# Zeroing a stage's semaphores in one block on five engines instead of one SyncE block per group

## The reference

```python
xn = _layernorm(x)
s = _L0_attn_ref(xn, ...)      # 16 heads of 16: W = (1e-4 + distance(Q, K)) ** -2, normalised, times V, gated
g = _silu(_L0_ffn_ref(xn, ...))  # ternary weights plus a low-rank part, squared ReLU, hidden 1024
x = x + s * g
xn = _layernorm(x)
s = _L1_attn_ref(xn, ...)      # W = (1 - arccos(cosine(Q, K)) / pi) ** 16, normalised, times V
g = _silu(_L1_ffn_ref(xn, ...))  # ternary weights, ReLU
x = x + s * g
```

## Time and profile before

| | us |
|---|---|
| median of 3 runs | 6679.3 |
| lowest and highest of them | 6676.99, 6679.74 |
| the profiled execution | 6678.16 |
| its span, first to last instruction | 6676.4 |
| ACT busy | 6177.6 (93%) |
| DVE busy | 5850.0 (88%) |
| POOL busy | 4185.5 (63%) |
| PE busy | 3870.0 (58%) |

### The profile page before, as it was taken

One profiled execution on the slowest core, in us unless ns is written; L12 is line 12 of the kernel. 1 busy time (PEld: TensorE's weight loads), 2 busy tenths in 40 slices (PEclk: granted clock), 3 DMA queues, 4 the chain that ended last, 5 costly groups with the idle time before them and its releaser, 6 DMA issues. The chain is left out here.

```text
span 6676.4 us, 49638 instructions
## 1 busy us (share of the span) xinstructions
PE 3870.0 (58%) x17072; PEld 1359.1 (20%) x17072; DVE 5850.0 (88%) x5940; ACT 6177.6 (93%) x1923; POOL 4185.5 (63%) x1127
## 2 busy tenths in 40 slices
PE   5777777777776764544454454444545444454545
PEld 2222222222222420111111121111112111111213
DVE  7867677767767679999999999999999999999996
ACT  3699999999999349999999999999999999999996
POOL 0399999999996006565565656556565656556563
PEclk8899999999998875566656665555656566665657
DMA  4311111111111420000000000000000000000003
GB/s 150 97 27 22 25 27 26 27 27 20 27 25 49 165 86 6 15 8 9 8 14 10 8 15 8 9 8 15 9 8 15 8 9 8 15 9 8 15 6 103
DMA packets 448852, 191.93 MB, mean 29 GB/s; under 512 B 348038, under 2 KB 429849, under 8 KB 446698
## 3 DMA queue, kind: packets, MB, share of 16 engines
q1 hardware_dynamic: 448618, 188.89, 11.1%
HBM read 112.52 MB, written 76.28 MB: 28 GB/s over the span
## 5 line engine op out<-in xcount | busy, mean ns | idle before, releaser
L1322 POOL TENSOR_TENSOR work<-work 128x1776 f32<-128x1776 f32 (+3 forms) x696 | 2149.0, 3088 | 55.3
L1114 PE MATMUL psS<-q_stack,k_stack 96*128 96x512 bf16 x2048 | 1034.0, 607 | 1761.0 <-DVE work L1230 1695.4
L981 POOL TENSOR_TENSOR work<-work 128x4096 f32<-128x4096 f32 x249 | 1737.7, 7013 | 152.6 <-ACT work L886 152.6
L896 DVE TENSOR_SCALAR work<-psS 128x1024 f32<-128x1024 f32 x1024 | 1198.1, 1218 | 555.0 <-PE psS L798 553.6
L1319 POOL TENSOR_SCALAR work<-work 128x1776 f32<-128x1776 f32 (+2 forms) x174 | 290.8, 1671 | 1990.6 <-ACT work L1204 1983.3
L1225 DVE TENSOR_SCALAR work<-psS 128x1024 f32<-128x1024 f32 x1024 | 1205.0, 1218 | 42.2 <-PE psS L1114 18.1
L1230 DVE TENSOR_TENSOR work<-psS,work 128x1024 f32<-128x1024 f32 x1024 | 1200.8, 1214 | 0.0
L1236 DVE SCALAR_TENSOR_TENSOR work<-work 128x2048 f32<-128x2048 f32 x512 | 1139.1, 2283 | 30.2 <-ACT work L1200 30.2
L1196 ACT ACTIVATE work<-work 128x2048 f32<-128x2048 f32 (+2 forms) x259 | 910.7, 3565 | 53.9 <-DVE work L1230 53.8
L1204 ACT ACTIVATE work<-work 128x6144 f32<-128x6144 f32 (+2 forms) x174 | 907.8, 5217 | 32.1 <-DVE work L1236 32.1
L1200 ACT ACTIVATE work<-work 128x2048 f32<-128x2048 f32 (+1 forms) x343 | 916.0, 2741 | 1.0
(11 more groups left out here) (139 smaller groups left out, 3398.0 us busy)
## 6 DMA issues: line engine op xcount, KB each, us to landing
qk_parts<-work SPq DMA_DIRECT2D x64, 384.0 KB, 3.3
q_stack<-qk_parts SPq DMA_DIRECT2D x384, 64.0 KB, 2.3
k_stack<-qk_parts SPq DMA_DIRECT2D x384, 64.0 KB, 2.3
xT_store<-work SPq DMA_DIRECT2D x2, 4096.0 KB, 15.8
v_store<-work SPq DMA_DIRECT2D x16, 512.0 KB, 3.3
v_tile<-v_store SPq DMA_DIRECT2D x64, 128.0 KB, 2.8
ffn_in<-xT_store SPq DMA_DIRECT2D x64, 128.0 KB, 2.7
y_store<-ffn_out SPq DMA_DIRECT2D x64, 128.0 KB, 2.4
```

What stands on the lines that cost most here:

```text
L896: nc.vector.tensor_scalar(lane(g)[:, 0, half * 1024:(half + 1) * 1024], m.psS[half][:, :], ZERO_SHIFT, None, ALU.max).then_inc(s_gd, 1)
L981: nc.gpsimd.tensor_tensor(lane(g, 2), lane(g, 2), lane(g, 2), ALU.mult).then_inc(s_wp, 1)
L1114: last = nc.tensor.matmul(m.psS[half][:, q * 512:(q + 1) * 512], m.k_stack[b][0:ROWS, kt * P:(kt + 1) * P], m.q_stack[b][0:ROWS, c:c + 512 ...
L1322: nc.gpsimd.tensor_tensor(part, part, part, ALU.mult).then_inc(s_pp, 1)
```

## The change

`sems` no longer registers a clear. It adds its semaphores to a list of the stage (`Phase.made`), and `Phase.block()` registers a single `clear` for the whole list just before it opens the stage's block. `clear` deals the list out: every fifth semaphore to SP, and likewise to DVE, ACT, PE and POOL, in one block. All seven stage functions use `Phase` in place of `ExitStack`.

```diff
+class Phase(ExitStack):
+    def __init__(self, nc):
+        super().__init__()
+        self.nc, self.made = nc, []
+    def block(self):
+        self.callback(clear, self.nc, self.made)
+        return self.enter_context(self.nc.Block())
 def sems(nc, ctx, prefix, *names):
     made = [ctx.enter_context(nc.semaphore(f"{prefix}_{n}")) for n in names]
-    ctx.callback(clear, nc, made)
+    ctx.made.extend(made)
     return made
...
     with nc.Block() as block:
         @block.sync
         def _(sp):
-            for s in made:
+            for s in made[0::5]:
                 sp.sem_clear(s)
+        @block.vector
+        def _(dve):
+            for s in made[1::5]:
+                dve.sem_clear(s)
+        @block.scalar
+        def _(act):
+            for s in made[2::5]:
+                act.sem_clear(s)
+        @block.tensor
+        def _(pe):
+            for s in made[3::5]:
+                pe.sem_clear(s)
+        @block.gpsimd
+        def _(pool):
+            for s in made[4::5]:
+                pool.sem_clear(s)
...
-    with ExitStack() as ctx:
+    with Phase(nc) as ctx:
...
-        block = ctx.enter_context(nc.Block())
+        block = ctx.block()
```

## The result

The changed kernel takes 6664.19 us (median of 17 runs) against 6678.56 us for the kernel before (17 runs): 14.4 us less. The ratio is 0.9978, with a 95% interval from 0.9971 to 0.9985. The profiled execution's span went from 6676.4 to 6661.9 us, 14.5 us less. One of the 17 runs of the changed kernel took 8298.85 us (granted clock 1.0), and one of the later runs of the kernel before took 8308.47 us; the ratios are taken without these two.

The account below looks back on a forecast made before the run. Eleven stretches between stages, 22.48 us with no engine at work, were taken to lie on the path. Handshakes of 3.85 us plus PE's clears of 3.7 us replace them, 14.9 us less: 6664.4 us, range 6660.0 to 6669.5 us.

Parts of the forecast that it names:

- What bounds: Eleven stretches between stages, 22.48 us with no engine at work; each microsecond cut there is one off the end.
- Rival 4: Stretches of norm and output stages hidden behind older work; about 6 us of the gain go, 6670.4 us; chance 0.03.
- The prices on SP: In the clear blocks between stages, 0.25 us per block besides its clears and 0.056 us per clear on SP.
- The floor: Least time of a clear block's handshake, however little SP does: 0.35 us each, 3.85 us for eleven blocks.
- The price of a clear on PE: PE, taken to finish each clear block last: 0.090 us per clear, 41 clears, 3.7 us.
- rival 1: Clears dear on PE or another engine: 0.18 us each gives 6668.1 us; verdict line crossed at 0.13 us; chance 0.14.
- The sum: Eleven stretches: 3.85 + 3.7 = 7.55 us in place of 22.48 us, 14.9 us less, median 6664.4 us.
- Rival 2: Shorter PE gaps keep TensorE's clock up at two stage boundaries; another 3.8 us won, 6660.6 us; chance 0.06.
- Rival 3: Jumps into and out of new clear bodies wait for code, 22 x 2.3 = 50.6 us; 6715.0 us; chance 0.03.
- The argument from the earlier trace: Against rival 3: DVE's first-norm-stage loops jump back repeatedly while the instruction queue moves a single packet in 50 us.
- The rule in the Trainium skill: About 51 ns per always-taken branch; 22 branches in a row on one engine would add 1.1 us; not added.

Follow-up runs that it names:

- merging alone: Against the kernel before: one clear block behind each stage, SP zeroing all 219 semaphores alone; 6671.21 us, ratio 0.9990.
- without PE: Against the changed kernel: each stage's semaphores dealt over four engines, SP, DVE, ACT and POOL; 6666.25 us in a single run.
- dealing out alone: Against the kernel before: its 40 clear blocks kept, each dealt over five engines; 6675.0 us, ratio 0.9995.

## Why the prediction was right, point by point

**What bounds.** The stretches were taken to be wholly on the path. Six kernels with stretches from 0.9 to 30 us bear it out. Against the 22.5 us of before, the stretches changed by -21.6, -13.5, -6.9, -3.1 and +7.7 us, and the medians by -23.1, -14.4, -7.2, -3.4 and +7.9 us. The medians move a little more each time, by 0.2 to 1.5 us. That lies within the intervals, and I leave it open. Rival 4 is out. (Its list took the stretch at 6620.25 us for that of an output stage; it follows the attention of layer 1. With the output stage's 2.84 us in place of 3.16 the price of that rival is still about 6 us.)

**The prices on SP.** 0.25 us for a block and 0.056 us for a clear gave 15.0 us for merging alone; 15.59 were measured, with one step of 0.38 us in it. These terms hold.

**The floor.** 0.35 us, put down to PE. The changed kernel's first stretch, with one clear on PE, takes 0.47 us, and the third, with two, 0.56 us. Less 0.117 us for each clear these are 0.35 and 0.33 us (DVE ends the first of them, 0.03 us behind PE). It holds.

**The price of a clear on PE** is the term that was mis-sized: 0.090 us was chosen, 0.117 to 0.12 us measured. I had taken the 34 ns by which PE's wait lasts longer than SP's as the whole difference. A clear on PE lasts 31 ns more than on SP (56 against 25), but another 30 ns lie around it that no duration shows. The 0.027 us by which the price was too low make 1.1 us for 41 clears. It stayed short of the 0.13 us from which rival 1 would have decided, but not by much: with the stall, all that the stretches hold over the floor is 5.1 us, where the line lay at 5.2.

**The sum.** 7.55 us were forecast for the stretches and 8.99 measured. The price on PE accounts for 1.1 us of the difference and the stall on DVE for 0.5 us, which together is 0.15 us too much. The saving in the stretches was thus 13.5 and not 14.9 us. The median still landed 0.2 us from the forecast, for two reasons that the prediction had no hold on: the median moved 0.9 us more than the stretches, which I can't assign, and the median of before came out at 6678.56 us over 17 runs, 0.7 us under the 6679.3 from which the forecast starts. The last microsecond of agreement is luck, the mechanism is not.

**Rival 2, a warmer TensorE,** named a real effect with the wrong cause. Single stages with TensorE in them move by 1 to 2 us, but in the same kernel from one execution to the next, in either direction, and the shortest output stage stands behind the longest stretch.

**Rival 3, code to be fetched.** Not at each branch: 40 places with five bodies show no such thing. But something of this family exists, 0.4 us at a fixed place in a queue, and one of the eleven stretches caught it. My price from the quickest transfer, 2.3 us, was five times too high. The argument from the earlier trace rows counted one instruction queue only. The same window has a packet on a second one, so two packets moved in those 50 us and not one:

```profile
q8 instruction: 1, 0.02, 0.1%
q14 instruction: 1, 0.01, 0.0%
```

The branches themselves left no trace in any sum. The rule in the Trainium skill that I weighed (Advanced Engine Details and Errata, section Control Flow Timing), an estimated 1.1 us here, would have brought the sum of the stretches nearer to the measured one, 8.65 against 8.99 us, but by accident. It is not what happened: the excess is in the steps between clears and in one stall. The floor of 0.35 us is the same for a block without a body on PE and, in the first stretch of the changed kernel, for one with a body and its two branches.

## What to carry to other kernels

Count the handshakes and the small queue instructions between stages, since they appear in no busy share: a window cut between two stages shows them as a stretch with nothing in it, and here each microsecond in such a stretch was one at the end. Look at the step of each engine before dealing queue instructions out: in one block behind each stage, all of them on PE lost 7.9 us, all on SP won 7.2 us, and an even deal over five engines won 14.4 us. A deal weighted by the steps was not run. Better still, put them beside other work: moving them off the path won 1.6 times what merging and dealing out had won. Judge a change of 0.2% by medians and by the stretches that it touches, because stages with TensorE in them vary by as much as 2 us each between executions of one kernel.

## What the runs showed of the hardware that was not expected

A clear takes a different time on each engine: from one to the next 0.06 us on SP, 0.07 us on ACT and on POOL, 0.09 us on DVE and 0.12 us on PE, with 56 ns of the last shown as its duration. An engine's queue can stand still for 0.4 to 0.5 us at a fixed place of its instruction stream; the stall repeated in the changed kernel at the same instruction (1.17 us in both stretches), stood there in the kernels without PE and with dealing out alone too (1.17 us each), and moved by two instructions when two were put in ahead.
